# Graph attention layer on one core: one stored mask row for eight heads, nodes loaded behind their own store, a sort stage and a logit copy moved

## What is computed

```python
for h in range(8):                                   # 8 heads of 64
    feat = x @ W[h]
    logit = leaky_relu((feat @ a1)[src] + (feat @ a2)[dst], 0.2)
    m = segment_max(logit, src)
    e = exp(logit - m[src])
    att = e / segment_sum(e, src)[src]
    out_h = relu(segment_sum(att[:, None] * feat[dst], src))
```

## Time and profile before

| | |
|---|---|
| median of 3 runs | 2954.81 us (2952.81 to 2958.27) |
| the profiled execution | 2949.85 us |
| its span in the trace | 2947.7 us |
| first gather of the layer to its last | 341.1 to 1484.0 us |
| granted TensorE clock, mean over the span | 0.958 |

### The profile page before, as it was taken

The page is one execution under the profiler, slowest core; times in us unless marked ns, Lnnn a source line. Parts: engine busy times, 40 slices in busy tenths (PEclk is TensorE's granted clock), DMA queues, the critical chain, the costliest instruction groups (busy, mean ns, idle before and its releaser), DMA issues. The chain is left out here.

```text
span 2947.7 us, 44087 instructions
## 1 busy us (share of the span) xinstructions
PE 2477.8 (84%) x10647; PEld 1532.7 (52%) x10692; DVE 2087.8 (71%) x3728; ACT 1208.1 (41%) x3972; POOL 1848.2 (63%) x1881
## 2 busy tenths in 40 slices
PE   5998479898898889898868888888888989999990
PEld 3565267676677677677656733333333333334440
DVE  8988678888988988888988565444444444445668
ACT  5943467777777677777745500000000000002220
POOL 0000267777777777777746367777777777774658
PEclk8999789999999999999989899999999999999995
DMA  6111478788888887888748867777777777773227
GB/s 210 60 49 41 123 223 243 236 243 234 238 242 235 240 234 239 235 239 241 234 148 261 299 196 210 210 210 210 210 209 210 209 210 210 210 210 119 66 57 298
DMA packets 243546, 589.44 MB, mean 200 GB/s; under 512 B 57744, under 2 KB 82832, under 8 KB 243400
## 3 DMA queue, kind: packets, MB, share of 16 engines
q0 software_dynamic: 133120, 443.52, 51.3%
q1 hardware_dynamic: 110280, 144.14, 14.9%
HBM read 533.43 MB, written 54.10 MB: 199 GB/s over the span
## 5 line engine op out<-in xcount | busy, mean ns | idle before, releaser
L557 POOL DMA_INDIRECT big<-feat_table,idx x880 | 850.0, 966 | 631.0 <-ACT idx L582 337.2
L1210 POOL DMA_INDIRECT big<-h_table,idx x784 | 742.0, 946 | 306.2 <-issue 269.9
L608 ACT ACTIVATE big<-big,late_weights 128x65 f32<-128x65 f32 x2640 | 644.9, 340 | 0.0
L870 PE MATMUL psA<-big,onehot 128*128 128x260 f32 x1760 | 437.4, 392 | 10.4 <-issue 1.5
L870 PE MATMUL psB<-big,onehot 128*128 128x260 f32 x1760 | 431.5, 388 | 4.3 <-DVE acc L753 0.5
L582 ACT CAST idx<-late_keys 128x8 int32 (+1 forms) x101 | 20.1, 203 | 944.9 <-DMA big<-h_table,idx 944.9
L870 PEld LDWEIGHTS psA<-big,onehot 128*128 128x128 f32 x1760 | 317.8, 190 | 93.0 <-issue 51.6
L870 PEld LDWEIGHTS psB<-big,onehot 128*128 128x128 f32 x1760 | 317.0, 190 | 56.4 <-issue 10.0
L1651 DVE TENSOR_TENSOR acc<-acc,psCD 128x512 f32 x176 | 120.5, 684 | 210.3 <-PE psCD L1966 208.2
L1651 DVE TENSOR_TENSOR acc<-acc,psA 128x512 f32 x176 | 120.5, 685 | 203.3 <-PE psA L1966 200.6
L1965 PE MATMUL psCD<-big,onehot 128*128 x352 | 185.1, 607 | 50.1 <-ACTq L1366 47.3
(11 more groups left out here) (465 smaller groups left out, 3796.1 us busy)
## 6 DMA issues: line engine op xcount, KB each, us to landing
nodes_all<-slot_nodes SPq DMA_DIRECT2D x56, 512.0 KB
big<-feat_table,idx POOLq DMA_INDIRECT x880, 3.9
feat_table<-big SPq DMA_DIRECT2D x49, 264.0 KB, 2.1
x_table<-acc SPq DMA_DIRECT2D x49, 256.0 KB, 5.9
h_table<-big SPq DMA_DIRECT2D x49, 256.0 KB, 3.9
big<-h_table,idx POOLq DMA_INDIRECT x784, 3.7
big<-h_table SPq DMA_DIRECT2D x49, 256.0 KB, 2.6
big<-x_table SPq DMA_DIRECT2D x49, 256.0 KB, 4.1
```

The costliest lines, as they stand in the source:

```text
L557: g.indirect_dma_start(ring[:, b.k, q * SB + u, :], None, feat_table, bass.IndirectOffsetOnAxis(ap=idx[:, 2 * b.k + q, u:u + 1], axis=0)). ...
L608: ins = s.activation(part, part, ACT.Copy, scale=late_weights[:, at:at + 1])
L870: ins = pet.matmul(psum[:, 512 * hf:512 * hf + HALF_W], onehot[:, q, u % SB, :], ring[:, b.k, u, HALF_W * hf:HALF_W * (hf + 1)], start=(u ...
L1210: g.indirect_dma_start(big[:, place:place + D], None, h1_table, bass.IndirectOffsetOnAxis(ap=idx[:, r.c % CHUNK_CYCLE, b:b + 1], axis=0)). ...
```

## The change

The mask row of an edge is stored once, and no longer for each head; the load of the masks of two batches becomes 8 loads, one for each head, of 16 partitions each. The store of `slot_nodes` has a semaphore of its own, `nodes_stored`, and the first nodes are loaded behind that one alone; the masks and `chunk_marks` still wait for the rest and for `look_ready`. In `feed` on ScalarE the copy of the `dst` logits stands between the late pairs 5 and 6, and no longer behind both. On VectorE the last of a batch's late sort stages stands behind `carry_runs` and the second one-hot matrix, ahead of `find_tops`. ScalarE's last clearing of the accumulator waits for the two semaphores in place of the one.

```diff
-        mask_table = nc.dram_tensor("mask_table", (P * SB * H, P), BF16).ap()
+        mask_table = nc.dram_tensor("mask_table", (P * SB, P), BF16).ap()
...
-        MASKS_16 = 32
+        MASKS_16 = 16 * (H + 1)
...
-            sp.dma_start(breaks[:, :, 0:P], mask_table[bass.ds(b(P, 0), 2 * P), :].rearrange(
-                "(k p) c -> p k c", p=P)).then_inc(masks_in, 16)
+            for h in range(H):
+                sp.dma_start(breaks[h::H, :, 0:P], mask_table[bass.ds(b(CH, 0), 2 * CH), :].rearrange(
+                    "(k c) p -> c k p", c=CH)).then_inc(masks_in, 16)
...
         def layer0_sync(sp):
-            sp.wait_ge(slots_stored, 16 * (1 + H + 2))
+            sp.wait_ge(nodes_stored, 16)
+            load_nodes(sp, batch(0))
+            sp.wait_ge(slots_stored, 16 * (1 + 2))
             sp.wait_ge(look_ready, 1)
-            load_nodes(sp, batch(0))
             load_masks_of_two(sp, batch(0))
...
             def feed(b, this=None):
                 if this:
-                    for a in range(OWN, LB - 1):
-                        weigh_late(this, a)
+                    weigh_late(this, OWN)
                 for n in range(ARRIVAL_GROUPS):
                     act.wait_ge(rows_arrived[b.k * ARRIVAL_GROUPS + n], b.pair(16 * ARRIVAL_GROUP, 16 * ARRIVAL_GROUP))
                 act.sem_inc(hold, 1)
                 wait_count(act, weights_turned, b(1, 0))
                 s.copy(dst_logit.rearrange("p (c h) -> p c h", h=H), ring[:, b.k, :, ACC_W:ROW_W]).then_inc(dst_kept, 1)
+                if this:
+                    for a in range(OWN + 1, LB - 1):
+                        weigh_late(this, a)
                 act.wait_ge(logit_done, b(1, 1))
...
                         if a == 5:
                             make_onehotT(aft, 1)
+                            if this and late.stages.get(this.c):
+                                late_stage(*late.stages[this.c][-1])
                             find_tops(nxt)
...
-                            for j, step, at in late.stages.get(this.c, ()):
+                            for j, step, at in late.stages.get(this.c, ())[:-1]:
                                 late_stage(j, step, at)
...
-            sp.dma_start(slot_nodes, oh_flat.bitcast(BF16)[:, 0:COLS]).then_inc(slots_stored, 16)
+            sp.dma_start(slot_nodes, oh_flat.bitcast(BF16)[:, 0:COLS]).then_inc(nodes_stored, 16)
             sp.wait_ge(masks_ready, 2)
-            copies = mask_table.rearrange("(r b h) p -> r b h p", b=SB, h=H)
-            for h in range(H):
-                sp.dma_start(copies[:, :, h, :], break_rows.rearrange("r (b p) -> r b p", p=P)).then_inc(slots_stored, 16)
+            sp.dma_start(mask_table.rearrange("(r b) p -> r b p", b=SB), break_rows.rearrange("r (b p) -> r b p", p=P)
+                         ).then_inc(slots_stored, 16)
...
-                act.wait_ge(slots_stored, 16 * (1 + H + 2))
+                act.wait_ge(nodes_stored, 16)
+                act.wait_ge(slots_stored, 16 * (1 + 2))
```

More of the change, by code:

```diff
@@ L279, in build @@
         slots_stored = sem("slots_stored")
+        nodes_stored = sem("nodes_stored")
         row_end = sem("row_end")
```

## The result

The changed kernel takes 2972.62 us (median of 6 runs, 2960.91 to 2981.07), the kernel before, measured beside it, 2953.81: a ratio of 1.0065 [1.0051, 1.0079]. It is 19 us slower where 21 less were forecast. The profiled execution took 2960.91 us and is the fastest of the six; that of before took 2949.85, so the traces show 11 us of the loss. What the slower executions spend beyond it no trace of this kernel shows.

A forecast was written before the change was run, and what follows sets the result against it. Two engines were taken as nearly equal bounds: VectorE with ScalarE at 20.6 to 20.7 us a batch, GpSimd at 20.40. Terms -10.8 - 10.7 - 1.1 + 1.6 = -21.0 gave 2934 us; forecast 2929 to 2939, 8-in-10 range 2926 to 2946.

The forecast's parts named there:

- Start, -10.8: Ahead of the third batch: earlier nodes remove GpSimd's 11.10 us wait, less the usual 0.30; first line 681 near 367.3.
- Eight mask loads at 0: On SyncE: eight issues at 0.59 take 4.7 us, masks land with 5 us to spare, so cost 0.
- Rival 4: Mask loads come late at 1.75 us an issue: +113 less the start's 11, 3057 us; chance 0.03.
- Loop, -10.7: The 847 gather intervals from the third batch: 1079.9 us against 1090.6; bounds -7.4 and -31.8.
- GpSimd at 20.40 when it is let free: Gathers of batches 3 to 10: GpSimd's own floor, 20.40 us a batch without a stall, becomes the loop's bound.
- Rival 3: In the loop, long gathers go away too as engines change phase: up to -43, say -32, 2923 us; chance 0.08.
- what is saved is only the round trip to TensorE, 0.58 us: ScalarE's earlier logit copy hides that trip under 16 weighings; a batch without stages goes from 19.77 to 19.2 us.
- Rival 5: Nothing won: the later layer gives back the gain; no clock or wait seen that would; chance 0.03.
- Tail, -1.1: From the last gather to the last line 681: 8.3 us after the change, 9.4 before.
- Ring and small stalls, +1.6: Ring from line 681 through lot 7, gather and landing to the next: 20.1 us, under 20.40; stalls 0.03 a batch.
- rival 2: Rows late: a landing of 4.6, not 3.9, makes the ring 20.7 in the mean; 2950 us; chance 0.10.
- Signs: In the new trace: VectorE waits for ScalarE's logit copy nearly everywhere, ScalarE for rows, showing GpSimd bounds.

The follow-up runs named there:

- Run 5: The changed kernel with the sort stage and ScalarE's order both put back, so only tables, their loads and early nodes changed: 2938.18 us, 0.9957.
- run 2: The kernel before with the moved sort stage on VectorE alone: 2957.76 us, 1.0022.
- run 1: The changed kernel with the last late sort stage put back in its old place on VectorE: 2966.66 us, 1.0048.
- run 6: The kernel before with ScalarE's new order alone: 2976.64 us, 1.0096.
- run 10: The changed kernel with ScalarE's order alone put back, the sort stage still moved: 2950.28 us, 0.9989.
- run 7: The changed kernel with 24 small matmuls ahead of `sum_ends`, filling TensorE's long wait: 2958.61 us, 1.0025.
- run 9: The changed kernel with the sort stage put back and 24 matmuls filling TensorE's long wait; ScalarE's new order stays: 2944.14 us, 0.9970.
- run 8: The changed kernel with one-column copies out of PSUM on VectorE ahead of the moved stage and between its two instructions: 2951.81 us, 0.9997.
- run 11: The changed kernel with ScalarE's order put back and one-column PSUM copies ahead of and inside the moved stage: 2937.55 us, 0.9943.
- run 4: The changed kernel with the moved stage further up, right behind `carry_runs`, ahead of lot 4's add and the second one-hot matrix: 2975.83 us, 1.0082.
- run 12: Run 11 with 24 matmuls ahead of `turn_logits` on TensorE: 2934.17 us, 0.9942.

## Why the prediction was wrong, step by step

**Start, -10.8: right.** Run 5 keeps the loop at before's 1090.6 and has 13 us less. Nodes were issued at 347.7 (351.4 in the sum), the first line 686 came at 367.21, and the wait of 11.10 went.

**Eight mask loads at 0: right.** The first eight take SyncE 5.10 us where 4.7 were reckoned, and no instruction of VectorE waits for them in run 5. Rival 4 is out. The Trainium skill's rule of joining small transfers (DMA: Bandwidth & Descriptors, Rules for kernel authors), from which 16 us were estimated beside it, has no sign in run 5 either: the eight were issued in 5.10 us, so SyncE did not wait out one before the next.

**Loop, -10.7: wrong, and it is here that the forecast failed.** Two steps of it did.

First: "GpSimd at 20.40 when it is let free". I took the gather time, long gathers included, as something the change does not touch, and gave it only bounds that were gains (-7.4 and -31.8). The moved stage itself makes gathers longer: in the same 847 intervals they cost 49.8 us beyond the median, where 20.40 a batch allows for 21.2. That is 28.6 of the 36.4 us by which the loop missed; the waits (8.1) are the rest. Rival 3 had the right quantity in view, the long gathers, but only with the other sign. The stage did leave VectorE's path as I wrote: in run 2 GpSimd's waits are gone. But GpSimd was the bound by then, and its own pace got worse by more than the waits had cost.

Second: "what is saved is only the round trip to TensorE, 0.58 us". I followed the copy to its reader and not on to what TensorE does next. With the `dst` logits early, TensorE turns them, does lot 4 at once and then stands ahead of `sum_ends`, since line 686 wants the logit copy behind 16 more weighings. Before, it stood twice, at `turn_logits` and at `sum_ends`; the kernel before on TensorE:

```profile
952.42 0.49 PE L839 MATMUL psCD<-ident_wide,look_space 128*128 128x128 f32 x2 [0.64 <-ACT look_space L620]
956.31 0.23 PE L843 MATMUL psCD<-look_space,head_of 128*8 128x32 f32 x2 [1.65 <-DVE look_space L686]
```

The two became one, in the changed kernel of 2.3 us and more in 21 batches, and behind some of these the clock falls (18 long lots). (At `sum_ends` TensorE waits for 144 us over the layer of before, 259 now.) The sum had no term for this, only the gain of 0.58 us a batch. In runs 1 and 6, where GpSimd is not the bound, it costs 27 us (against run 5) and 25 (against before); in the changed kernel run 10 against it says 22 by the ratios, though the two traces' loops are only 13 apart. Runs 7 and 9 show that most of it is the idle time in one piece and not the order as such: the same order with the gap filled gets back 12 and 23 us, and some 4 us stay with the order. Rival 5's sentence "I see no clock or wait that would" was written for the later layer; I had not asked it of this one.

The Trainium skill (TensorE: Matmul & The Clock Gate, HAM oscillation — how this bites in real kernels) describes a loop in which TensorE waits for operands in each tile and comes back at half clock each time. The trace of the changed kernel agrees in part: its 18 long lots stand behind waits, at a granted clock of 0.53 to 0.86, on an engine that is 88% busy, but most batches have none. Had I set that page of the Trainium skill against the moved copy, it would have been the rival of the other sign that I lacked: run 6 prices it.

**Tail, -1.1: right within 0.3.** From the last gather to the last line 686 it takes 1506.08 - 1497.48 = 8.6 us, 8.3 were forecast.

**Ring and small stalls, +1.6:** the ring is not what stalls. Landing has a median of 3.8, so rival 2 is out too.

**Signs.** Of those named in the prediction, VectorE waits for ScalarE's logit copy in 52 of 55 batches (14 before), and ScalarE for rows 54 times, 1.85 us each: GpSimd bounds the loop, as forecast. I read this sign as a gain to come; it only says who is the bound, and not at what pace.

**What stays open.** How VectorE stretches a gather, and why two copies of one column ease it. The Trainium skill (SBUF — State Buffer, Who interferes with whom) says that VectorE and GpSimd share one pair of ports under an exclusive lock, taken by VectorE's copies and `tensor_scalar` in a two-port mode, and by two-input instructions only against GpSimd's reads; its section on SBUF's two separate sides says that GpSimd can't write the descriptors of its transfers while VectorE runs in such a mode. The traces agree in that a row of VectorE's SBUF instructions, two-input ones among them, can hold a gather until it is over. They add that the moment of the start decides: in the changed kernel the four begun within 0.1 us of the start of such a one-hot instruction took 0.95 us. In the loop of before no gather under the one-hot matrix takes over 1.20 us, and two stages in a row ahead of line 681 (the one at 931.40 is in the earlier trace rows) make 1.46 at most:

```profile
931.44 1.46 POOL L557 DMA_INDIRECT big<-feat_table,idx  x1 [0.30 <-issue]
```

It is the two kinds side by side that made 2.33. Whether the copies of runs 8 and 11 help because they read PSUM or only because they part the instructions is not shown: in run 4 the add, which reads PSUM too, stood between and did not help. Whether the gather is held by its read or its write was not tried. And that the changed kernel's median stands 8 us further above its profiled execution than before's does is not explained.

The best versions found are run 12 and run 11, 0.9942 [0.9927, 0.9957] and 0.9943 [0.9925, 0.9961], and run 5 at 0.9957 [0.9944, 0.9971], which their intervals don't tell apart: the tables' edits alone hold nearly all of the gain.

## What to carry to other kernels

When an edit makes a software-driven queue such as GpSimd's gathers the bound, its own pace is a term of the sum: look which gathers are long now and what VectorE does beside them, and price the moved instructions as neighbours, both up and down. When a copy is moved ahead, follow it past its reader to that engine's next wait: the same idle time in one piece can cost a step of the clock that it did not cost in two. Edits in one diff want a kernel each, since here -13 (the tables), +9 (the stage on top of them) and +22 (ScalarE's order on top of both) hid in one +19. The three add up by construction; in another order ScalarE's would be 25 or 27.

## What was unexpected of the hardware

- A gather of 0.95 us took 2.26 when it began 0.24 us after the start of a one-hot instruction with a sort stage right behind it, and ended 0.8 us after the stage. There were 17 such gathers; over the layer all gathers together took 31 us more.
- TensorE ran a lot of 1.97 us in 2.9 to 3.7 us after 1.8 to 3.2 us of idle time, with a mean load of 88% around it, though not after every such wait; 24 small matmuls (1.5 us) in that gap removed all such lots.
- Sixteen long lots cost most of 23 us where TensorE was waited for (run 1 against 9), and five cost nothing that shows where GpSimd bounded the loop (run 11 against 12).
- Eight loads of 8 KB in place of one of 64 KB took SyncE 5.10 us to issue and cost the loop nothing that shows: 965 ns a gather and 1090.6 us in run 5, 966 and 1090.6 before.
